# Routing of a mixture-of-experts layer in three parts instead of two, in a fused transformer block

## The reference, cut to what matters

```python
h = prelu((d_gamma * (q @ k.T)) @ v @ Wo + bo)          # token mixing
h = h + attention(layernorm(h))                          # 8 heads, head size 8, relative bias, softmax
# the last stage, which the change touches
xn = layernorm(h) * gamma + beta
logits = xn @ Wr + br                                    # 8 experts
top_vals, top_idx = top_k(logits, 2)
w_full = sum(softmax(top_vals)[k] * one_hot(top_idx[k])) # weight of each expert for each token
for e in range(8):
    y += (gelu(xn @ W1[e] + b1[e]) @ W2[e] + b2[e]) * w_full[..., e]
out = h + y
```

## Time and profile before

| what | us |
|---|---|
| median of 3 runs | 582.22 (581.95 to 583.33) |
| the profiled execution, its own time | 577.09 |
| its span, first to last instruction | 575.3 |
| PE busy | 528.6 (92%) |
| DVE busy | 456.7 (79%) |
| ACT busy | 356.3 (62%) |
| POOL busy | 76.7 (13%) |

### The profile page before, as it was taken

The page is one execution under the profiler, slowest core; times in us unless marked ns, Lnnn a source line. Parts: engine busy times, 40 slices in busy tenths (PEclk is TensorE's granted clock), DMA queues, the critical chain, the costliest instruction groups (busy, mean ns, idle before and its releaser), DMA issues.

```text
span 575.3 us, 12938 instructions
## 1 busy us (share of the span) xinstructions
PE 528.6 (92%) x4240; PEld 179.0 (31%) x4240; DVE 456.7 (79%) x526; ACT 356.3 (62%) x627; POOL 76.7 (13%) x179
## 2 busy tenths in 40 slices
PE   7999899557999999999999999999999994999996
PEld 4333233221333333333333333333333431232221
DVE  2666677878999999999999999999998646566653
ACT  2021222323889898888989888898988452435442
POOL 9600010203110000101000010100003320010000
PEclk9999999965999999999999999999999896999999
DMA  7900268373232232323323232322342000000000
GB/s 260 245 15 2 49 207 238 101 219 94 55 85 79 74 86 58 89 72 83 77 70 83 61 88 72 82 78 66 86 127 71 11 11 30 22 0 19 19 19 18
DMA packets 51095, 46.33 MB, mean 81 GB/s; under 512 B 26265, under 2 KB 39034, under 8 KB 51066
## 3 DMA queue, kind: packets, MB, share of 16 engines
q1 hardware_dynamic: 51066, 45.94, 29.0%
HBM read 29.75 MB, written 16.17 MB: 80 GB/s over the span
## 4 chain that ended last, share of the span: by engine, by line
PE 67%; DVE 6%; DMA 1%; issue 1%; ACT 1%; SPq 1%; POOL 1%; DVEq 0%
PE ps L1405 24%; PE ps L1315 13%; PE ps L1390 12%; PE ps L1538 5%; PE ps L1564 5%; DVE nmax L869 2%; PE ps L1394 1%; PE ps L1420 1%; PE ps L1329 1%; PE ps L1551 1%; DVE probs L1141 1%; DMA maxima<-max_t 1%; SPq L411 1%; PE ps L1561 1%; PE ps L1445 1%
## 5 line engine op out<-in xcount | busy, mean ns | idle before, releaser
L869 DVE TENSOR_REDUCE nmax<-ps 128x1 f32<-128x1024 f32 x256 | 302.0, 1219 | 18.4 <-PE ps L1315 9.2
L729 ACT ACTIVATE probs<-ps 128x512 f32<-128x512 f32 x512 | 278.0, 596 | 59.5 <-PE ps L1390 49.4
L1405 PE MATMUL ps<-probs,v_ring 128*32 128x256 f32 x2048 | 165.3, 395 | 0.0
L1315 PE MATMUL ps<-k_ring,q_ring 48*128 48x512 bf16 x512 | 102.9, 399 | 6.8 <-DVE nmax L869 6.8
L1390 PE MATMUL ps<-q_ring,k_ring 51*128 51x512 bf16 x512 | 102.7, 386 | 5.9 <-DMA q_ring<-maxima 1.6
L749 ACT ACTIVATE probs<-ps,wide_w 128x1024 f32<-128x1024 f32 x32 | 35.5, 1114 | 43.5 <-PE ps L1538 41.4
L1141 DVE TENSOR_TENSOR probs<-probs,ps 128x1024 f32<-128x1024 f32 x32 | 39.1, 1221 | 29.3 <-PE ps L1551 26.2
L1315 PEld LDWEIGHTS ps<-k_ring,q_ring 48*128 48x128 bf16 x512 | 24.7, 93 | 113.5 <-issue 101.3
L1405 PEld LDWEIGHTS ps<-probs,v_ring 128*32 128x32 f32 x2048 | 40.7, 108 | 61.7 <-issue 37.2
L889 DVE TENSOR_TENSOR gated<-ps,gamma_sb 128x1024 f32<-128x1024 f32 x32 | 38.7, 1220 | 11.2 <-PE ps L1235 11.2
L1390 PEld LDWEIGHTS ps<-q_ring,k_ring 51*128 51x128 bf16 x512 | 30.8, 93 | 46.1 <-issue 23.6
(11 more groups left out here) (160 smaller groups left out, 333.2 us busy)
## 6 DMA issues: line engine op xcount, KB each, us to landing
k_ring<-qk_parts SPq DMA_DIRECT2D x64, 96.0 KB, 2.4
q_ring<-qk_parts SPq DMA_DIRECT2D x64, 96.0 KB, 2.4
gamma_sb<-gamma_t SPq DMA_DIRECT2D x4, 1024.0 KB, 11.0
v_padded<-v_pad SPq DMA_DIRECT2D x4, 1024.0 KB, 4.6
v_ring<-v_padded SPq DMA_DIRECT2D x32, 128.0 KB, 3.2
outputs<-o_t SPq DMA_DIRECT2D x32, 128.0 KB
qk_parts<-qk_h SPq DMA_DIRECT2D x8, 384.0 KB, 4.4
x_ring<-bias_parts SPq DMA_DIRECT2D x32, 96.0 KB, 3.2
```

Of the source, the lines that this page charges most:

```text
L729: A.activation(probs[:, s % 4, HALF * j:HALF * (j + 1)], ps[:, key_bank(s, j), :], ACT.Exp).then_inc(exp_done[j], 1)
L869: V.tensor_reduce(nmax[:, par, s:s + 1], ps[:, bank:bank + 2, :].rearrange("p a n -> p (a n)"), AX, ALU.max, negate=True).then_inc(s1_redu ...
L1315: return mm(ps[:, bank + j, :], q_ring[rows, u, P * s:P * (s + 1)], k_ring[rows, u, HALF * j:HALF * (j + 1)], start=True, stop=(s > 0 or j ...
L1405: last = mm(ps[VC * j:VC * (j + 1), PVB, 0:2 * P], v_ring[:, u, m, :], probs[:, m % 4, 2 * P * j:2 * P * (j + 1)], start=(m == 0), stop=(m ...
```

## The change: three parts of routing

Routing now has three parts (`PHASES`): batch 0, batches 1 and 2, and batch 3. Batch 0's logits are made in step (3, 0) and turned in (3, 2) of the last head, and its routing on VectorE is interleaved with the norm of batches 1 and 2. Its exponential is made on ScalarE behind step 6 of the last head. Only batch 0's weights (four transposes) are turned behind up(0). The second part's first choice and second highest logit stand ahead of unit 0's product on VectorE, the rest behind the products of units 0, 4, 5 and 6; its exponential is now GpSimd's, on 16 tiles. Its weights (eight transposes) are turned in unit 7 and copied by ScalarE. Batch 3's steps come one unit later than before, with other grouping. In the split, one set of four instructions takes the place of two.

```diff
-    TILES = (slice(0, (B - 1) * NT), slice((B - 1) * NT, B * NT))
+    PHASES = (slice(0, 1), slice(1, B - 1), slice(B - 1, B))
+    TILES = tuple(slice(p.start * NT, p.stop * NT) for p in PHASES)
...
+            exp_gap(1)
             scale_attention(B - 1)
             square_late(B - 1)
             power(2 * B - 1)
-            exp_gap(1)
+            exp_gap(2)
...
+                        if last and (u, s) == (RING - 1, NT - 2):
+                            act.wait_ge(gap_ready, 1)
+                            A.activation(e_gap[:, TILES[0]], gap[:, TILES[0]], ACT.Exp).then_inc(e_gap_ready, 1)
...
-            act.wait_ge(gap_ready, 1)
-            A.activation(e_gap[:, TILES[0]], gap[:, TILES[0]], ACT.Exp).then_inc(e_gap_ready, 1)
...
+            def weights_copy(h):
+                batches = PHASES[h]
+                n = batches.stop - batches.start
+                act.wait_ge(w_turned, h + 1)
+                A.activation(wt[:, batches, :].rearrange("p b n -> p (b n)"), ps[:, 7, :].bitcast(bf16)[:, 0:n * HALF],
+                             ACT.Copy).then_inc(w_t_copied, n)
+            WITHIN = {E - 1: (weights_copy, 1), E + 1: (leave_ye, 0), E + 4: (norm_copy, B - 1),
+                      E + 6: (logits_copy, B - 1), 2 * E + 1: (leave_ye, 1), 2 * E + 5: (weights_copy, 2),
+                      3 * E + 1: (leave_ye, 2)}
...
+            def second_choice(h):
+
                 V.tensor_tensor(tiles(gap, h), tiles(top2, h), tiles(top1, h), ALU.subtract).then_inc(gap_ready, 1)
+                pick_first(hot2, h)
...
             def route_parts(h):
+                p0, p1, p2 = (w_p[:, PHASES[h], :, :, E * i:E * (i + 1)].rearrange("p b c j e -> p (b c j) e")
+                              for i in range(PARTS))
+                full, rest = tiles_e(w_full, h), tiles_e(w_rest, h)
+                step(V.tensor_copy(p0, full))
+                step(V.tensor_tensor(rest, full, p0, ALU.subtract))
+                step(V.tensor_copy(p1, rest))
+                V.tensor_tensor(p2, rest, p1, ALU.subtract).then_inc(w_split, 1)
...
+            for stage, arg in ((add_residual, 0), (center, 0), (add_residual, 1), (center, 1), (variance, 0),
+                               (add_residual, 2), (scale, 0), (variance, 1), (norm_affine, 0), (center, 2),
+                               (scale, 1), (logits_copy, 0), (variance, 2), (norm_affine, 1), (logits_bias, 0),
+                               (first_choice, 0), (scale, 2), (second_top, 0), (norm_affine, 2), (second_choice, 0),
+                               (logits_copy, 1), (two_weights, 0), (all_weights, 0), (route_parts, 0), (logits_bias, 1),
+                               (weights_copy, 0), (first_choice, 1), (second_top, 1)):
+                stage(arg)
...
-            WITHIN = {1: [(invert_sums, B - 1)], E - 1: [(add_residual, B - 1), (center, B - 1)],
-                      E: [(variance, B - 1)], E + 1: [(scale, B - 1)], E + 6: [(route_first, 1)],
-                      E + 7: [(route_second, 1)], 2 * E: [(route_weights, 1)], 2 * E + 1: [(route_parts, 1)]}
+            WITHIN = {0: [(second_choice, 1)], 2: [(invert_sums, B - 1)], 4: [(two_weights, 1)], 5: [(all_weights, 1)],
+                      6: [(route_parts, 1)], E: [(add_residual, B - 1), (center, B - 1)], E + 1: [(variance, B - 1)],
+                      E + 2: [(scale, B - 1)], E + 7: [(logits_bias, 2), (first_choice, 2)],
+                      E + 8: [(second_top, 2), (second_choice, 2)], 2 * E + 2: [(two_weights, 2), (all_weights, 2)],
+                      2 * E + 3: [(route_parts, 2)]}
...
+                if b == B - 1:
+                    pe.wait_ge(w_t_copied, B - 1)
...
-                      (2, 4): [(project_attention, 2)], (2, 6): [(turn_norm, 0)], (3, 1): [(turn_norm, 1), (logits, 0)],
-                      (3, 3): [(turn_norm, 2), (logits, 1)], (3, 5): [(logits, 2)], (3, 7): [(turn_logits, 0)]}
+                      (2, 4): [(project_attention, 2)], (2, 6): [(turn_norm, 0)], (3, 0): [(logits, 0)],
+                      (3, 1): [(turn_norm, 1)], (3, 2): [(turn_logits, 0)], (3, 3): [(turn_norm, 2), (logits, 1)],
+                      (3, 5): [(logits, 2)], (3, 7): [(turn_logits, 1)]}
...
                 if k == 0:
                     pe.wait_ge(res_seq, B - 1)
+                    pe.wait_ge(lg_t_copied, 2)
                 if k == 1:
-                    pe.wait_ge(w_t_copied, B - 1)
+                    pe.wait_ge(w_t_copied, 1)
+                    pe.wait_ge(lg_read, B - 1)
...
-            WITHIN = {E - 1: (project_attention, B - 1), E + 1: (finish, 0), E + 3: (turn_norm, B - 1),
-                      E + 4: (logits, B - 1), E + 6: (turn_logits, 1), 2 * E + 1: (finish, 1),
-                      2 * E + 3: (turn_weights, 1), 3 * E + 1: (finish, 2)}
+            WITHIN = {E - 1: (turn_weights, 1), E: (project_attention, B - 1), E + 1: (finish, 0),
+                      E + 4: (turn_norm, B - 1), E + 5: (logits, B - 1), E + 7: (turn_logits, 2),
+                      2 * E + 1: (finish, 1), 2 * E + 4: (turn_weights, 2), 3 * E + 1: (finish, 2)}
```

More of the change, by code:

```diff
@@ L1022, in _ @@
             attend_dve(G // RING - 1, False, True)
[L1025 to L1028, removed]
             step = chain(route_seq, 0)
@@ L1039, in over_e, with find_top, pick_first @@
                 return tiles(m, h).rearrange("p (m o) -> p m o", o=1).to_broadcast([P, TILES[h].stop - TILES[h].start, E])
-            def first_of(logits, top, hot, h):
+            def find_top(logits, top, h):
                 step(V.tensor_reduce(tiles(top, h), tiles_e(logits, h), AX, ALU.max))
                 step(V.tensor_tensor(tiles_e(eq, h), tiles_e(logits, h), over_e(top, h), ALU.is_equal))
+            def pick_first(hot, h):
                 step(V.tensor_tensor(tiles_e(eq, h), tiles_e(eq, h), tiles_e(rank, h), ALU.mult))
@@ L1061, in route_first, with logits_copy @@
[L1061 to L1071, removed]
+            def logits_copy(h):
+                rows, bank = (slice(0, P), 3) if h else (slice(0, UPPER), 0)
+                dve.wait_ge(routed, 1 + 2 * h)
+                V.tensor_copy(lg_t[rows, h, :], ps[rows, bank, :]).then_inc(lg_t_copied, 1)
@@ new lines, in logits_bias @@
+            def logits_bias(h):
+                first, n = PHASES[h].start, PHASES[h].stop - PHASES[h].start
+                dve.wait_ge(lg_turned, h + 1)
+                for b in range(first, first + n):
+                    lg_v = ps[:, (0, 1, 7)[h], 0:2 * P * n].rearrange(
+                        "p (c t x) -> p c t x", t=2 * n, x=VC)[:, :, 2 * (b - first):2 * (b - first) + 2, 0:E]
+                    br_v = br_b.rearrange("p (c t e) -> p c t e", c=1, t=1).to_broadcast([P, NT // 2, 2, E])
+                    V.tensor_tensor(lg[:, NT * b:NT * (b + 1), :].rearrange("p (c t) e -> p c t e", t=2), lg_v, br_v,
+                                    ALU.add).then_inc(lg_read, 1)
@@ L1088, in route_parts @@
             def route_parts(h):
[L1090 to L1101, removed]
@@ L1102, in route_parts @@
-                last.then_inc(w_split, 1)
-            def weights_copy():
-                dve.wait_ge(w_turned, 1)
-                V.tensor_copy(wt[:, 0:B - 1, :].rearrange("p b n -> p (b n)"),
-                              ps[:, 0:2, :].rearrange("p a n -> p (a n)").bitcast(bf16)[:, 0:(B - 1) * HALF]
-                              ).then_inc(w_t_copied, B - 1)
-            for k in range(2):
-                logits_copy(k)
-            route_first(0)
-            route_second(0)
-            route_weights(0)
@@ new lines, in weights_copy @@
+            def weights_copy(b):
+                dve.wait_ge(w_turned, 1)
+                V.tensor_copy(wt[:, b, :], ps[:, 0, :].bitcast(bf16)[:, 0:HALF]).then_inc(w_t_copied, 1)
+            for stage, arg in ((add_residual, 0), (center, 0), (add_residual, 1), (center, 1), (variance, 0),
[5 more added lines that the diff above has]
+                stage(arg)
@@ L1449, in turn_logits @@
             def turn_logits(h):
-                if h == 0:
-                    pe.wait_ge(lg_t_copied, 1)
-                    turn_four(0, lg_t[:, 0, :], lg_turned)
-                pe.wait_ge(lg_t_copied, 2 + h)
+                pe.wait_ge(lg_t_copied, 1 + h)
+                if h == 1:
+                    pe.wait_ge(xf_ready, B - 1)
+                    turn_four(1, lg_t[:, 1, :], lg_turned)
+                    return
                 for c in range(NT // 2):
-                    last = nc.tensor.transpose(ps[:, 7 if h else 1, 2 * VC * c:2 * VC * (c + 1)],
-                                               lg_t[0:UPPER, 0 if h else 1, P * c:P * (c + 1)],
-                                               ident[0:UPPER, 0:UPPER])
+                    last = nc.tensor.transpose(ps[:, 7 if h else 0, 2 * VC * c:2 * VC * (c + 1)],
+                                               lg_t[0:UPPER, 0, P * c:P * (c + 1)], ident[0:UPPER, 0:UPPER])
                 last.then_inc(lg_turned, 1)
@@ L1463, in turn_weights @@
```

(9 more changed lines are left out.)

36 lines of the change are left out of this document (13 added, 23 removed).

## The result

The changed kernel takes 573.83 us, the median of 4 runs (572.23 to 574.07), against 582.76 for the kernel before beside it (581.95 to 583.33). The ratio is 0.984, 95% interval 0.982 to 0.987, so 8.9 us or 1.5% less. The time of 573.83 itself is still inside the range, by 0.2; the gain, taken against the kernel before beside it, lies just beyond it, and well beyond the forecast. A second set of runs gave 575.08 against 582.99, ratio 0.988 (0.983 to 0.993): 7.9 us by the medians, which is inside the range. Medians and ranges of times are of all runs here, while the ratios leave out executions in a slower state of the core.

A forecast was written before the change was run, and what follows sets the result against it. TensorE was taken as the bound, with time to win only where it idles behind the last head. The terms -8.35 + 1.8 + 0.55 + 0.5 gave -5.5 us, so 576.7 us from 582.22, range 573.6 to 578.9.

The forecast's parts named there:

- What bounds the kernel: TensorE idle or slow behind the last head; at stake the 18.16 us from turned logits to first down's end.
- The last head: Batch 0's logits and first choice ahead of scale(2) on VectorE: turned logits 0.6 us later, at 474.0.
- To the first down: From the turned logits to the first down's end at 483.2, against 491.55: 8.35 us earlier, at full clock.
- Unit 0: Second choice behind product 0: GpSimd's `pow` holds up VectorE's two-input step, so TensorE waits 1.8 us before spread(2).
- The first rival: At unit 0's second choice `pow` does not hold VectorE up: 7.8 us less, 574.4 us; chance 0.33.
- Units 2 to 7: Routing steps behind these units' products fit into VectorE's free time: no cost.
- The change of batch: Around units 7 to 11, eight transposes and a longer ScalarE copy: down(6) to up(11) 8.95 us, 0.5 lost.
- Units 15 to 20: Batch 3's routing one unit later, three steps beside `pow`: net loss 0.5 us, zero without the exclusion.
- The second: One extra half-clock stretch, from TensorE's waits in the last head and first units: 578.4 us; chance 0.14.
- The third: Clock stays low through units 0 to 7, 2.2 us more each; 585.5 us with four such units; chance 0.04.

The follow-up runs named there:

- e7: The changed kernel with the second part's second choice, weights and split put ahead of unit 0's product on VectorE; median 582.33 us, ratio 1.002 to the kernel before.
- e6: The changed kernel with scale(2) ahead of batch 0's first choice and batch 2's affine step ahead of its second top; median 574.95 us, ratio 0.985.
- e3: The changed kernel with one GpSimd multiplication of 128x512 added ahead of the second part's `pow`; one run, 576.94 us.
- after: The changed kernel as first measured and profiled; its profile took 573.97 us, the median of its 4 runs is 573.83 us.
- e2: The changed kernel, unchanged, run again for its spread; six runs of 569.68 to 579.39 us, the profile at 569.68 us.
- e9: The changed kernel with the second part's weights one unit earlier on VectorE, behind products 3 and 4; one run, 573.11 us.

## Why the prediction was wrong, point by point

**What bounds the kernel: right.** The gap behind the last head was the place, and e7 shows that what stands ahead of the first product is paid in full.

**The last head: right.** +0.6 forecast, +0.4 measured; the reason given (scale(2) behind the first choice) is the one that e6 takes away.

**To the first down: right in kind, 0.45 short.** From the turned logits it was forecast at 9.2 us (474.0 to 483.2) and is 8.8 in both profiles. The steps of VectorE came out nearly as priced (0.28 to 0.29 and a pitch of 0.32 on 16 tiles, 0.42 for the copy). Some 0.25 of the surplus lies ahead of them: I added pauses to values, up(0) and turning, which the chain gives without any (1.00, 1.06 and 0.34). The rest is spread over the copy and the eight steps (2.50, forecast 2.6).

**Unit 0: the step that failed.** The forecast had `pow` hold up the second choice, product 1 end 2.6 us later for it, and spread(2) wait 1.8 us; this is the term of 1.8 in the sum. `pow` on 16 columns takes 2.90 (3.1 forecast), but L1050 beside it takes 0.29, product 1 follows at once, and spread(2) stands in the chain without a wait, so the term is 0. The rows for it were of a multiplication on 512 columns. e3 shows that this one does exclude the same step, so the inference from an operation of one kind and size to another was the fault. The Trainium skill ("SBUF — State Buffer", "Who interferes with whom") has the exclusion of a VectorE instruction with two SBUF inputs for any GpSimd instruction that reads SBUF; the multiplications agree with it, and the three profiles of `pow` (2.90 us, steps of 0.28 to 0.29 beside it in after, e2 and e7) do not, so here the measurement decides. The first rival, at 0.33, was the one that came true.

**Units 2 to 7: a collision missed.** "No cost" was wrong: the exclusion that I had put in the wrong place struck in unit 5, by GpSimd's multiplication. It cost 0.4 to 0.5 us: from the first down to the end of down(6) it is 14.18 us in after and 14.08 in e2, where before has 13.70, and e9 takes it away.

**The change of batch: right.** Forecast 8.95 us from the end of down(6) to up(11), against 8.5 before; it is 8.89 in after and in e2. So 0.4 of the 0.8 in the table belongs here, and the rest is unit 5's.

**Units 15 to 20: wrong for the same reason.** 0.5 forecast, -0.1 measured; `pow` beside the three steps of unit 16 does nothing.

**The sum.** With the exclusion struck out the forecast's own terms give -7.8, and -8.3 is measured in matched profiles. That is the mechanism of the first rival. That its 574.4 us is only 0.6 from the median of 573.83 is in part luck: 0.2 in the last head and 0.4 to the first down were won beyond the forecast, and the collision in unit 5, which it didn't have, took 0.4 to 0.5 back.

**The range.** It took the low side from the bounded prices alone and left out that the median of a few runs moves with the clock: the two comparisons of the same two kernels gave 8.9 and 7.9. The time of one kernel spans 577 to 589, and this was not in the three runs shown, though the 5.1 us between profile and median hinted at it. I passed over that gap instead of asking which stretch of the trace could be 5 us longer.

**The rivals of the clock.** The second (one extra half-clock stretch in the last head) happened in e3, at 1.5 us (forecast 1.7). The third (clock low through the first units) happened in no profile of after; in e7 the clock fell within 6.9 us without work, and in after the gaps of 0.4 to 0.9 us at the same place left it at 1.00.

## What to carry to other kernels

Splitting a serial chain paid here because every piece found idle time of its engine in the steady loop behind it: the first piece early brought nothing without the rest hidden (e7). Measure an exclusion between engines with the very operation that will stand there; here the exclusion by long multiplications said nothing about a short `pow`, and it moved with the schedule to where the long one landed. Where the profiled execution and the median differ by more than the runs do, compare kernels by stretches of profiles with the same granted clock, not by whole spans: here 3.1 us of span stood for 8 of time.

## What the runs showed of the hardware that I had not expected

The same program on one core took 576.7 to 588.7 us, and most of it goes with the mean granted clock (0.963 to 0.939), some 4 us for each 0.01. In the 14 profiles the half-clock time between 440 and 470 us is 3 to 24 us. TensorE is 86 to 95% busy there, with the attention projections (64 columns each) between score and value matmuls, and waits of up to 1.9 us.

GpSimd's `pow` takes 1.64 us on 8 columns and 2.90 on 16: by these two points an estimated 0.16 a column and 0.4 fixed. VectorE's steps with two SBUF inputs run beside it at their usual 0.29 on 16 tiles (after, e2, e7) and 0.22 on 8 (e2, unit 16). Beside a multiplication of 128x512 they end 0.15 after it (after, e2, e3). Whether it is the operation or the size that makes the difference wasn't told apart.
